# Zero-padded transposed probabilities in two half copies, and score masks in the scores' own tiles

## The chip, the cores and the metric

One NeuronCore of a Trainium2 chip runs the whole program. The metric is device time in microseconds (us), the median of the runs shown. Engines are named as the profile names them: PE is TensorE (PEld its weight loads), DVE VectorE, ACT ScalarE, POOL GpSimd, SP the engine that issues most DMAs. L540 is line 540 of the kernel before.

## The reference, cut to what matters

A "macaron" block on x of shape (2, 1024, 128): half an attention/feed-forward stack, a linear recurrence, half the same stack again. A stack has six layers, each of them

```
qkv = shift(x) @ Wqkv            # 16 heads of 64
q, k = l2norm and rotary tables
sim  = q . k over a window: 32 queries see their own 32 keys and the 32 before them
sim  = where(mask, -max, sim)    # no key after the query, none more than 32 before it
attn = softmax(sim)              # over 64 keys
x    = (attn @ v) @ Wo + x
x    = ffn(shift(x)) + x
```

A tile is 128 positions, which is four windows of 32. There are 16 tiles and 12 layers over the two stacks, so 192 tile-layers. Everything here is float32, except the mask and the identity that brings it in (`idb`), which are bfloat16.

## The kernel before, in words

Each engine runs its own program, unrolled over about 198 steps. In step s the tile-layer s-1 is projected (L_QKV), s-2 has its q and k transposed, its values computed and its scores taken (L_S), s-3 its softmax and the transposition of the probabilities (L_SM), s-4 its attention product and output projection (L_AV, L_WO), s-5 and s-6 its feed-forward (L_F, L_F2). The order inside a step is written out by hand for every engine; engines meet only through semaphores. `k.wait(sem, lag)` waits until `sem` has counted the tile of that lag.

The order on PE in one step is: projections 1 and 0 (L482), transposition of q (`tps`, L493), the attention product (`attend`, L540), projections 2 and 3, transposition of k, output projection (L593), transposition of the probabilities (L601), of the feed-forward's input (L606), the second feed-forward product (L621), the values (L488, second one after DVE's third rotation, L866), transposition of the next x (L639), the first feed-forward product (L501), the mask products (L517), the scores (L525).

The parts that the change touches:

- **Scores.** For each of 8 pairs of heads, two window halves `ty`, two windows `g` and two heads `hp` there is a product of 64 rows of contraction by 32 columns of output, so that it occupies one of eight 64x32 tiles of the array. They add onto a mask which two bfloat16 products of full 128x128 size (`idb` against a mask of 512 columns, one for each `ty`) have written to the two banks of `sps` before.
- **Probabilities.** After the softmax eight transpositions put them into PSUM (`tps`), partitions being keys (0 to 63 of one window pair, 64 to 127 of the other), and ACT copies all of it to `pT` in SBUF (L721).
- **Attention product.** 64 products of 64 rows by 64 columns, the moving operand 32 columns wide, take `pT` against the values (`va`) or the values shifted by one window (`vb`); the two window halves `t` go to two banks of `ops`. ACT copies `ops` to `oT` in another order (L695).
- **Next x.** PE transposes it into `tps` (slot 4; slot 5 for the recurrence's input) and waits before it for ACT's copies of k and of the probabilities, which read `tps`.
- **DVE's order.** Within a step: rotations, sums, the inverse square root in twelve small pieces (L815 to L847), between which it adds to `Z` (L968, L978), then the work of the recurrence in between the stacks (`middle`, 16 tiles only), then `hT` (L990, after ACT's gelu `fg`), then the maximum and subtraction of the scores (L997, L1000).
- **Instructions.** Every float32 product is recorded as two pairs of a weight load and a matmul, so the 64 products of `attend` and the 64 of `scores` are 128 pairs each in a step. PE's program is fetched by a DMA queue of its own (q8).

Of the kernel before, what the change touches and what calls it, by code (L numbers as in the profile page):

```python
# [21 lines left out]
P = 128  # L22
DEPTH, HEADS, DH, WIN = 6, 16, 64, 32
# [34 lines left out]
def macaron(nc, x_in, w_in, w_out, b_out, w_qkv, q_scale, k_scale, w_o,  # L58
            w_1, w_2, b_2, c_cols, c_rope, c_mask, c_ident, out):
    with ExitStack() as ctx:  # L60
# [13 lines left out]
        qT = sb("qT", [PAIRS, P])  # L74

        prob = sb("prob", [PAIRS, 2, 2 * WIN])
        pT = sb("pT", [PAIRS, P])
        oT = sb("oT", [PAIRS, P])
        va = sb("va", [2, INNER])
        vb = sb("vb", [INNER])  # L80
# [58 lines left out]
        d_vb = sem("d_vb")  # L139
        d_out = sem("d_out")  # L140
        c_zero, c_zero2 = sem("c_zero"), sem("c_zero2")
        s_idb, s_mask = sem("s_idb"), sem("s_mask")
        c_kf, c_scl = sem("c_kf"), sem("c_scl")
        c_sig = sem("c_sig")
# [321 lines left out]
        def _(pe):  # L466
# [45 lines left out]
            def scores(k):  # L512
                first = k.off("first", L_S, lambda u: ((POS - 1 - u % POS) // (POS - 1)) * 512)
                par = k.parity(L_S)
                for ty in range(2):
                    m = mask[:, bass.ds(first, 512)] if ty == 0 else mask[:, 0:512]
                    mm(sps[:, ty, :], idb[:, :], m, start=True, stop=False, skip_group_check=True)  # L517
                for p in range(PAIRS):
                    for ty in range(2):
                        for g in range(2):  # L520
                            for hp in range(2):
                                w = 2 * ty + g
                                at, rows = par * P + w * WIN, slice(hp * DH, (hp + 1) * DH)
                                to = (2 * g + (hp ^ ty)) * WIN
                                last = mm(sps[to:to + WIN, ty, p * 64:(p + 1) * 64], qT[rows, p, w * WIN:(w + 1) * WIN],  # L525
                                          kT[rows, p, at:at + 2 * WIN], start=False, stop=True, skip_group_check=True)
                last.then_inc(p_S, 1)

            def attend(k):
                par = k.parity(L_AV)  # L530
                for p in range(PAIRS):
                    for g in range(2):
                        for hp in range(2):
                            for t in range(2):
                                o4 = ops[:, t, p * 64:(p + 1) * 64].rearrange("p (g i) -> p g i", g=2)
                                at = (2 * p + hp) * DH
                                rows = slice(t * DH, (t + 1) * DH)
                                v = vb[rows, at:at + DH] if g == 0 else va[rows, par, at:at + DH]
                                to = (2 * g + (hp ^ t)) * WIN
                                last = mm(o4[hp * DH:(hp + 1) * DH, g, :], v, pT[rows, p, to:to + WIN],  # L540
                                          start=True, stop=True, skip_group_check=True)
                last.then_inc(p_O, 1)

            def step(k):
# [13 lines left out]
                    idle(4)  # L558
                if k.on(L_AV):
                    k.wait(a_pT, L_AV)  # L560
                    k.wait(d_vb, L_AV, per=32)
                    k.wait(v_z1, L_WO + 1)
                    k.wait(v_z, L_F2 + 1, base=TILES)
                    k.wait_mid(m_bh, M_IN + 1)
                    k.wait_mid(m_x2, M_OUT + 1)
# [63 lines left out]
                    k.wait(v_ab[2], L_QKV)  # L629
                    values(k, 0)  # L630
                if k.on(L_X):
                    k.wait(a_kT, L_S)
                    k.wait(a_pT, L_SM)
                    if k.mid(M_T) is not None:
                        k.wait_mid(m_xn, M_T)
                        tr(tps[:, 5, :], mx_n[:, :], idf[:, :])
                    k.wait(v_z, L_X)
                    k.wait_mid(m_z, TILES)
                    tr(tps[:, 4, :], Z[:, bass.ds(k.slot(L_X), P)], idf[:, :]).then_inc(p_xT, 1)  # L639
                if k.on(L_F):  # L640
                    k.wait(a_xnT, L_F)
                    if k.s == L_F:
# [25 lines left out]
        def _(act):  # L668
# [10 lines left out]
            def step(k):  # L679
                if k.on(L_QKV):  # L680
                    k.wait(v_red[0], L_QKV + 1)
                    square(k, 1)
                    square(k, 0)
                if k.on(L_SM):
                    k.wait(v_sub, L_SM)
                    fn(prob[:, :, :, :], prob[:, :, :, :], ACT.Exp).then_inc(a_exp, 1)
                if k.on(L_S):

                    k.wait(p_qT, L_S)
                    k.wait(p_S, L_S + 1)  # L690
                    cp(qT[:, :, :], tps[:, :, :]).then_inc(a_qT, 1)
                if k.on(L_AV):
                    k.wait(p_O, L_AV)
                    k.wait(p_wo, L_WO + 1)
                    cp(oT[:, :, :].rearrange("p a (t x) -> p t a x", t=2),  # L695
                       ops[:, :, :].rearrange("p t (a x) -> p t a x", x=2 * WIN)).then_inc(a_oT, 1)
                if k.on(L_QKV):
                    k.wait(v_red[1], L_QKV + 1)
                    square(k, 3)
                    square(k, 2)  # L700
                if k.on(L_S):
                    if k.parity(L_S) == 0:

                        k.wait(a_kT, L_S + 1)
                        k.wait(p_S, L_S + 1)
                        fl = k.off("flag", L_S, lambda u: u % TILES)
                        fn(kT[:, :, 0:WIN], kT[:, :, 2 * P:2 * P + WIN], ACT.Copy,
                           scale=kflag[:, bass.ds(fl, 1)]).then_inc(a_car, 1)
                    k.wait(p_kT, L_S)
                    k.wait(p_S, L_S + 1)  # L710
                    at = WIN + k.parity(L_S) * P
                    cp(kT[:, :, at:at + P], tps[:, :, :]).then_inc(a_kT, 1)
                if k.on(L_F):
                    k.wait(v_nb, L_F)
                    k.wait(p_xnT, L_F + 1)
                    fn(xn[:, :], xs2[:, :], ACT.Identity, bias=nb[:, 0:1], scale=rt2[:, 1:2]).then_inc(a_xn, 1)
                if k.on(L_SM):

                    k.wait(p_pT, L_SM)
                    k.wait(p_O, L_AV)  # L720
                    cp(pT[:, :, :], tps[:, :, :]).then_inc(a_pT, 1)  # L721
                if k.on(L_F):
                    k.wait(p_xnT, L_F)
                    k.wait(p_f[0], L_F + 1)
                    n = k.layer(L_F, 1)
                    fn(xnT[:, :], sps[:, 1, 0:P], ACT.Identity, bias=cols[:, RAW_B + n:RAW_B + n + 1],
                       scale=cols[:, RAW_G + n:RAW_G + n + 1]).then_inc(a_xnT, 1)
                if k.on(L_S):
                    k.wait(p_O, L_S + 2)
                    k.wait(d_vb, L_S + 1, per=32)  # L730
                    values(k, 1)
                    values(k, 0)
                if k.on(L_F):
                    k.wait(p_f[1], L_F)
                    k.wait(v_h, L_F + 1)
                    at = k.layer(L_F, 2)
                    for c in range(3):
                        rows = min(FC, FH - c * FC)
                        last = fn(fg[0:rows, c, :], proj[0:rows, 1, c * P:(c + 1) * P], ACT.Gelu,  # L739
                                  bias=cols[0:rows, bass.ds(at + c * 2 * DEPTH + 1, 1)])  # L740
                    last.then_inc(a_gelu, 1)
                if k.on(L_X):
                    k.wait(p_xT, L_X)
                    k.wait(p_v[0], L_X + 2)
                    hf, par = P // 2, k.parity(L_X)
                    cp(xsT[0:hf, par, 0:P], tps[0:hf, 4, :])
                    cp(xsT[hf:P, par, 1:P + 1], tps[hf:P, 4, :])
                    k.wait(a_xT, L_X + 1)
                    fn(xsT[hf:P, par, 0:1], xsT[hf:P, 1 - par, P:P + 1], ACT.Copy,
                       scale=0.0 if k.tile(L_X) % POS == 0 else 1.0).then_inc(a_xT, 1)  # L750
                if k.mid(M_T) is not None:

                    k.wait(p_xT, L_X)
                    cp(mx_t[:, :], tps[:, 5, :]).then_inc(m_xT, 1)

            def between(s):

# [24 lines left out]
        def _(dve):  # L782
# [135 lines left out]
            def step(k):  # L918
# [60 lines left out]
                if k.on(L_QKV):  # L979
                    for n in (8, 10, 11, 12):  # L980
                        rsqrt(k, n)
                middle(k)
                if k.on(L_F):
                    k.wait(p_f[0], L_F)
# [57 lines left out]
        def _(pool):  # L1042
# [99 lines left out]

            def between(s):

                if s in (1, 2):
                    outer_pow(1 + s)
                if s == 1:
# [26 lines left out]
def _constants():  # L1174
# [13 lines left out]
    rope = kinds.reshape(4, POS, P, DH).transpose(2, 0, 1, 3).reshape(P, 4 * POS * DH).astype(f)  # L1188

    row = np.arange(P)  # L1190
    i, g = (row % WIN)[:, None], (row // (2 * WIN))[:, None]
    j = (np.arange(512) % (2 * WIN))[None, :]
    usual = ((j < WIN) & (j >= i)) | ((j >= WIN) & (j - WIN <= i))
    first = np.where(g == 0, usual & (j >= WIN), usual)
# [22 lines left out]
```

## Time and profile before

| | |
|---|---|
| median of 3 runs | 3309.44 us (3306.02 to 3310.67) |
| the profiled execution's own time | 3317.88 us |
| its span, first to last instruction | 3316.0 us |
| busy share of the span | PE 96%, PEld 72%, DVE 83%, ACT 77%, POOL 67% |
| mean granted clock of TensorE | 0.995 of full speed |
| PE's two costliest helpers here | L540 378.6 + 376.7 us, L525 302.9 us |

A busy share is an average over stages: about 165 steps do only the layers' work, some 16 in the middle of the program do the recurrence besides, and the first and last few fill and drain the pipeline. Idle time is put before the instruction that waited, with the engine and line that ended it; "issue" means that nothing in the profile ended it.

### The profile page before, as it was taken

What the parts mean: (1) busy time and instruction counts of PE and PEld (TensorE: products, weight loads), DVE (VectorE), ACT (ScalarE), POOL (GpSimd) and SP (SyncE); (2) the same over time, 40 slices, a digit from 0 to 9 for tenths busy, and PEclk for the clock granted to TensorE, in tenths of its full rate; (3) what the DMA queues carried; (4) which work ended last, traced back from release to release, by engine and by line L of the source; (5) the groups of instructions that cost most, each with busy time, mean ns of one, the idle gap of its engine ahead of it and who ended that gap; (6) DMA issues with size and microseconds to landing.
All of it is one profiled execution on the core that took longest, in us unless ns stands there. A gap on an engine that the chain in (4) does not pass through costs nothing. (4 is left out here: it accounts for less than half of the span.)

```text
span 3316.0 us, 150147 instructions
## 1 busy us (share of the span) xinstructions
PE 3177.3 (96%) x63272; PEld 2384.7 (72%) x63464; DVE 2748.5 (83%) x6951; ACT 2545.5 (77%) x4144; POOL 2226.4 (67%) x1453
## 2 busy tenths in 40 slices
PE   7999999999999999999999999999999999999997
PEld 4777777777777777777777777777777777777776
DVE  7888888888888888889998888888888888888885
ACT  3777777777777777777777777777777777777775
POOL 6666666666666666667887666666666666666663
PEclk9999999999999999999999999999999999999999
DMA  4111111111111111111111111111111111111111
GB/s 124 45 48 45 48 44 48 45 48 45 47 42 43 48 45 48 45 48 45 47 39 45 48 44 48 45 46 41 45 48 45 48 44 48 45 44 43 47 52 38
DMA packets 135089, 157.39 MB, mean 47 GB/s; under 512 B 75539, under 2 KB 108439, under 8 KB 134423
## 3 DMA queue, kind: packets, MB, share of 16 engines
q1 hardware_dynamic: 129815, 144.42, 15.7%
q8 instruction: 509, 8.34, 1.1%
q10 hardware_dynamic: 4608, 3.34, 0.3%
q14 instruction: 157, 1.29, 0.1%
HBM read 33.38 MB, written 1.05 MB: 10 GB/s over the span
## 5 line engine op out<-in xcount | busy, mean ns | idle before, releaser
L1073 POOL TENSOR_TENSOR rot<-rot,swp 128x1024 f32<-128x1024 f32 x384 | 907.0, 2362 | 137.8 <-DVE rot L866 137.8
L482 PE MATMUL proj<-wq,xsT 128*128 128x512 f32 x1536 | 769.6, 622 | 27.6 <-DVE rot L866 10.3
L673 ACT ACTIVATE sq<-proj 128x512 f32<-128x512 f32 x768 | 438.0, 596 | 416.1 <-PE proj L482 406.3
L1082 POOL TENSOR_TENSOR rot<-rot,rn 128x1024 f32<-128x1024 f32 x384 | 724.4, 1908 | 0.0
L1063 POOL TENSOR_TENSOR rt<-rt,half 128x1 f32<-128x1 f32 x192 | 105.3, 549 | 755.6 <-DVE rt L936 755.6
L860 DVE TENSOR_TENSOR swp<-proj,tab 128x512 f32<-128x512 f32 x768 | 521.3, 679 | 12.2 <-ACT sq L673 7.2
L866 DVE TENSOR_TENSOR rot<-proj,tab 128x512 f32<-128x512 f32 x768 | 517.9, 674 | 0.8 <-PE tps L493 0.8
L990 DVE SCALAR_TENSOR_TENSOR hT<-proj,cols,fg 114x128 f32<-114x128 f32 (+1 forms) x576 | 166.7, 345 | 417.7 <-ACT fg L739 413.6
L493 PEld LDWEIGHTS tps<-idf,rot 128*128 128x128 f32 x3072 | 360.2, 141 | 206.2 <-issue 204.1
L1067 POOL TENSOR_TENSOR prob<-prob,rr 128x1024 f32<-128x1024 f32 x192 | 365.4, 1903 | 174.9 <-DVE rr L948 174.9
L482 PEld LDWEIGHTS proj<-wq,xsT 128*128 128x128 f32 x1536 | 259.8, 190 | 254.9 <-issue 145.4
L493 PE MATMUL tps<-idf,rot 128*128 128x128 f32 x3072 | 399.2, 273 | 2.8 <-POOL rot L1082 1.9
L540 PE MATMUL ops<-pT,vb 64*64 64x32 f32 x12288 | 378.6, 220 | 5.1 <-issue 4.9
L540 PE MATMUL ops<-pT,va 64*64 64x32 f32 x12288 | 376.7, 219 | 2.5 <-issue 2.3
L593 PE MATMUL ops<-wo,oT 128*128 128x128 f32 x3072 | 376.2, 276 | 2.4 <-ACT oT L695 2.4
L525 PEld LDWEIGHTS sps<-kT,qT 64*32 64x32 f32 x24576 | 260.0, 105 | 163.2 <-issue 163.0
L525 PE MATMUL sps<-kT,qT 64*32 64x64 f32 x24576 | 302.9, 225 | 71.6 <-issue 71.4
L488 PE MATMUL proj<-wq,xsT 128*128 128x512 f32 x768 | 367.8, 600 | 3.4 <-DVE rot L866 3.3
L593 PEld LDWEIGHTS ops<-wo,oT 128*128 128x128 f32 x3072 | 359.6, 193 | 2.7 <-issue 2.6
L540 PEld LDWEIGHTS ops<-pT,vb 64*64 64x64 f32 x12288 | 329.2, 134 | 38.2 <-issue 38.0
L721 ACT COPY pT<-tps 128x1024 f32<-128x1024 f32 x192 | 194.4, 1013 | 186.4 <-PE tps L601 186.4
L540 PEld LDWEIGHTS ops<-pT,va 64*64 64x64 f32 x12288 | 331.4, 135 | 3.2 <-issue 2.7
(102 smaller groups left out, 5873.0 us busy)
## 6 DMA issues: line engine op xcount, KB each, us to landing
vb<-va SPq DMA_DIRECT2D x192, 384.0 KB, 3.5
vb<-va SPq DMA_DIRECT2D x192, 128.0 KB, 3.6
wq<-in_L_ffn_Wqkv SPq DMA_DIRECT2D x95, 192.0 KB, 3.4
xs<-Z SPq DMA_DIRECT2D x192, 32.0 KB
wo<-in_L_ffn_Wo SPq DMA_DIRECT2D x94, 64.0 KB, 2.8
xs<-Z SPq DMA_DIRECT2D x192, 28.0 KB
xs<-Z SPq DMA_DIRECT2D x192, 3.8 KB
xs<-Z SPq DMA_DIRECT2D x192, 0.2 KB
```

Of the source, the lines that this page charges most:

```text
L482: mm(proj[:, c % 2, :], xsT[:, k.parity(L_QKV), 0:P], wq2[:, bass.ds(w + c * 512, 512)], start=True, stop=True).then_inc(p_qkv[c], 1)
L488: mm(proj[:, c, :], xsT[:, k.parity(L_S), 0:P], wq2[:, bass.ds(w + (4 + c) * 512, 512)], start=True, stop=True).then_inc(p_v[c], 1)
L493: last = tr(tps[:, p, :], rot[:, g * INNER + p * P:g * INNER + (p + 1) * P], idf[:, :])
L525: last = mm(sps[to:to + WIN, ty, p * 64:(p + 1) * 64], qT[rows, p, w * WIN:(w + 1) * WIN], kT[rows, p, at:at + 2 * WIN], start=False, stop ...
L540: last = mm(o4[hp * DH:(hp + 1) * DH, g, :], v, pT[rows, p, to:to + WIN], start=True, stop=True, skip_group_check=True)
L593: last = mm(ops[:, 0, 0:P], oT[:, p, :], wo[:, bass.ds(w + p * P, P)], start=(p == 0), stop=(p == PAIRS - 1))
L673: fn(sq[:, c * 512:(c + 1) * 512], proj[:, c % 2, :], ACT.Square).then_inc(a_sq[c], 1)
L860: v.tensor_tensor(halves(swp[:, c * 512:(c + 1) * 512]), swapped, tab[:, bass.ds(po + (2 * g + 1) * POS * DH, DH)] .rearrange("p (a d) -> ...
L866: v.tensor_tensor(heads(rot[:, c * 512:(c + 1) * 512]), heads(src), tab[:, bass.ds(po + 2 * g * POS * DH, DH)].unsqueeze(1) .to_broadcast( ...
L1067: g_.tensor_tensor(pr, pr, rr[:, :].unsqueeze(2).to_broadcast([P, HEADS, 2 * WIN]), ALU.mult).then_inc(g_nrm, 1)
L1073: g_.tensor_tensor(r, r, swp[:, g * INNER:(g + 1) * INNER], ALU.add).then_inc(g_add[g], 1)
L1082: g_.tensor_tensor(r, r, rn[:, g * HEADS:(g + 1) * HEADS].unsqueeze(2) .to_broadcast([P, HEADS, DH]), ALU.mult).then_inc(g_nm[g], 1)
```

## The change

The transposed probabilities get a buffer of twice the size, `pT[pair and g, hp, t, i]`. For half t = 0 only the partitions 0 to 63 are written, for t = 1 only 64 to 127, and the rest stays zero from one memset by POOL at the start. ACT copies the lower half of the partitions, DVE the upper half (in a new place, between the last piece of the inverse square root and `middle`), so that neither copy touches the zeros. Each product of `attend` then contracts over all 128 partitions and has a moving operand of 64 columns, the zeros cancelling what does not belong to it: 32 products of 128 rows by 64 columns instead of 64 of 64 by 64. PE waits for both copies. `ops` is filled in the order of `oT`. The next x is transposed into `ops` instead of `tps`, and PE waits for DVE's addition to `Z` instead of ACT's copies before it. The mask is written by eight products of 64 rows by 32 columns, each 512 wide, and the constant's rows are numbered to match.

```diff
-        pT = sb("pT", [PAIRS, P])
+        pT = sb("pT", [PAIRS * 2, 2, 2, WIN])
...
                 for ty in range(2):
                     m = mask[:, bass.ds(first, 512)] if ty == 0 else mask[:, 0:512]
-                    mm(sps[:, ty, :], idb[:, :], m, start=True, stop=False, skip_group_check=True)
+                    for g in range(2):
+                        for hp in range(2):
+                            rows, of = slice(hp * DH, (hp + 1) * DH), hp * DH + g * WIN
+                            to = (2 * g + (hp ^ ty)) * WIN
+                            mm(sps[to:to + WIN, ty, :], idb[rows, of:of + WIN], m[rows, :], start=True, stop=False,
+                               skip_group_check=True)
...
                 for p in range(PAIRS):
+                    o4 = ops[:, p // 4, (p % 4) * P:(p % 4 + 1) * P].rearrange("p (t g i) -> p t g i", t=2, g=2)
                     for g in range(2):
                         for hp in range(2):
-                            for t in range(2):
-                                o4 = ops[:, t, p * 64:(p + 1) * 64].rearrange("p (g i) -> p g i", g=2)
-                                at = (2 * p + hp) * DH
-                                rows = slice(t * DH, (t + 1) * DH)
-                                v = vb[rows, at:at + DH] if g == 0 else va[rows, par, at:at + DH]
-                                to = (2 * g + (hp ^ t)) * WIN
-                                last = mm(o4[hp * DH:(hp + 1) * DH, g, :], v, pT[rows, p, to:to + WIN],
-                                          start=True, stop=True, skip_group_check=True)
+                            at = (2 * p + hp) * DH
+                            v = vb[:, at:at + DH] if g == 0 else va[:, par, at:at + DH]
+                            last = mm(o4[hp * DH:(hp + 1) * DH, :, g, :], v,
+                                      pT[:, 2 * p + g, hp, :, :].rearrange("p t i -> p (t i)"),
+                                      start=True, stop=True, skip_group_check=True)
...
                     k.wait(a_pT, L_AV)
+                    k.wait(v_pT, L_AV)
...
                 if k.on(L_X):
-                    k.wait(a_kT, L_S)
-                    k.wait(a_pT, L_SM)
+                    k.wait(v_z1, L_WO)
...
-                    tr(tps[:, 4, :], Z[:, bass.ds(k.slot(L_X), P)], idf[:, :]).then_inc(p_xT, 1)
+                    tr(ops[:, 0, P:2 * P], Z[:, bass.ds(k.slot(L_X), P)], idf[:, :]).then_inc(p_xT, 1)
...
-                    cp(pT[:, :, :], tps[:, :, :]).then_inc(a_pT, 1)
+                    if k.s == L_SM:
+                        act.wait_ge(c_pz, 1)
+                    cp(pT[0:DH, :, :, 0, :], tps[0:DH, :, :].rearrange("p c (g h i) -> p (c g) h i", g=2, i=WIN)).then_inc(a_pT, 1)
...
                     for n in (8, 10, 11, 12):
                         rsqrt(k, n)
+                if k.on(L_SM):
+
+                    if k.s == L_SM:
+                        dve.wait_ge(c_pz, 1)
+                    k.wait(p_pT, L_SM)
+                    k.wait(p_O, L_AV)
+                    src = tps[DH:P, :, :]
+                    swapped = bass.AP(src.tensor, src.offset + WIN,
+                                      [list(src.ap[0]), [2 * WIN, 2 * PAIRS], [-WIN, 2], [1, WIN]])
+                    v.tensor_copy(pT[DH:P, :, :, 1, :], swapped).then_inc(v_pT, 1)
                 middle(k)
...
+                if s == 0:
+                    g_.memset(pT[:, :, :, :, :], 0.0).then_inc(c_pz, 1)
```

## Rows read from the trace of the kernel before

**Rows 1.** The page, part 1: busy us, share of span, instructions.
```profile
PE 3177.3 (96%) x63272; PEld 2384.7 (72%) x63464; DVE 2748.5 (83%) x6951; ACT 2545.5 (77%) x4144; POOL 2226.4 (67%) x1453
```
**Rows 2.** Waits of the whole run: who waited <- for whom: us in total, times, longest.
```profile
DVE hT L990 <- ACT fg L739: 413.6, 179, 4.2
...
PEld proj L488 <- DVE rot L866: 96.4, 189, 1.1
DVE mx L997 <- PE sps L525: 71.4, 70, 3.9
```
**Rows 3.** Timeline of DVE, ordinary step: start us, us, [idle before <-releaser].
```profile
835.24 0.87 DVE L990 SCALAR_TENSOR_TENSOR hT<-proj,cols,fg 114x128 f32<-114x128 f32 x3 [2.31 <-ACT fg L739]
...
846.82 0.68 DVE L866 TENSOR_TENSOR rot<-proj,tab 128x512 f32<-128x512 f32 x1
...
847.51 0.28 DVE L968 TENSOR_TENSOR Z<-Z,ops 128x128 f32<-128x128 f32 x1
...
849.11 0.19 DVE L847 SCALAR_TENSOR_TENSOR rn<-rt,sps 128x32 f32<-128x32 f32 x1
851.66 0.61 DVE L990 SCALAR_TENSOR_TENSOR hT<-proj,cols,fg 114x128 f32<-114x128 f32 x2 [2.36 <-ACT fg L739]
```
**Rows 4.** Timeline of ACT, the same step.
```profile
846.28 1.01 ACT L721 COPY pT<-tps 128x1024 f32<-128x1024 f32 x1 [0.81 <-PE tps L601]
...
848.78 0.59 ACT L677 COPY va<-proj 128x512 f32<-128x512 f32 x1 [0.19 <-PE proj L488]
849.38 1.28 ACT L739 ACT_TABLE_LOAD   x1
```
**Rows 5.** Timeline of PE, the same step and the one before.
```profile
830.38 1.93 PE L488 MATMUL proj<-wq,xsT 128*128 128x512 f32 x4
...
834.26 1.48 PE L525 MATMUL sps<-kT,qT 64*32 64x64 f32 x128
...
838.61 0.32 PE L540 MATMUL ops<-pT,vb 64*64 64x32 f32 x8
...
840.61 0.70 PE L482 MATMUL proj<-wq,xsT 128*128 128x512 f32 x1
...
846.86 1.88 PE L488 MATMUL proj<-wq,xsT 128*128 128x512 f32 x4
...
848.73 1.60 PE L501 MATMUL proj<-xnT,w 128*114 128x128 f32 x12
...
850.69 1.48 PE L525 MATMUL sps<-kT,qT 64*32 64x64 f32 x123
```
**Rows 6.** Timeline of PE, scores of a stalled step; then the page's instruction queue.
```profile
2416.27 1.28 PE L525 MATMUL sps<-kT,qT 64*32 64x64 f32 x104
2419.08 0.43 PE L525 MATMUL sps<-kT,qT 64*32 64x64 f32 x24 [1.53 <-issue]
...
q8 instruction: 509, 8.34, 1.1%
```
**Rows 7.** The recurrence's stretch: stage busy times; DVE's longest wait there.
```profile
1543.00:1825.00 282.00, 272.05 (x5342) 205.54 (x5357) 269.54 (x702) 215.50 (x358) 226.16 (x184) 1.00 0.16 44
...
DVE hT L990 <- ACT fg L739: 6.4, 5, 1.5
```
**Rows 8.** Groups by line: busy us, mean ns of one | idle before.
```profile
L540 PEld LDWEIGHTS ops<-pT,va 64*64 64x64 f32 x12288 | 331.4, 135 | 3.2 <-issue 2.7
L525 PEld LDWEIGHTS sps<-kT,qT 64*32 64x32 f32 x24576 | 260.0, 105 | 163.2 <-issue 163.0
L860 DVE TENSOR_TENSOR swp<-proj,tab 128x512 f32<-128x512 f32 x768 | 521.3, 679 | 12.2 <-ACT sq L673 7.2 <-issue 4.9
L1000 DVE TENSOR_TENSOR prob<-sps,mx 128x1024 f32<-128x1024 f32 x192 | 235.0, 1224 | 6.6
L1015 DVE MEMSET va<- 128x1024 f32 x1 | 0.9, 912 | 0.2 <-issue 0.2
L1126 POOL MEMSET hT<- 128x384 f32 x1 | 0.4, 417 | 0.0
```

More of the change, by code:

```diff
@@ L141, in macaron @@
         c_zero, c_zero2 = sem("c_zero"), sem("c_zero2")
+        c_pz = sem("c_pz")
+        v_pT = sem("v_pT")
         s_idb, s_mask = sem("s_idb"), sem("s_mask")
@@ L631, in step @@
                 if k.on(L_X):
-                    k.wait(a_kT, L_S)
-                    k.wait(a_pT, L_SM)
+                    k.wait(v_z1, L_WO)
                     if k.mid(M_T) is not None:
                         k.wait_mid(m_xn, M_T)
-                        tr(tps[:, 5, :], mx_n[:, :], idf[:, :])
+                        tr(ops[:, 0, 2 * P:3 * P], mx_n[:, :], idf[:, :])
                     k.wait(v_z, L_X)
                     k.wait_mid(m_z, TILES)
-                    tr(tps[:, 4, :], Z[:, bass.ds(k.slot(L_X), P)], idf[:, :]).then_inc(p_xT, 1)
+                    tr(ops[:, 0, P:2 * P], Z[:, bass.ds(k.slot(L_X), P)], idf[:, :]).then_inc(p_xT, 1)
                 if k.on(L_F):
@@ L694, in step @@
                     k.wait(p_wo, L_WO + 1)
-                    cp(oT[:, :, :].rearrange("p a (t x) -> p t a x", t=2),
-                       ops[:, :, :].rearrange("p t (a x) -> p t a x", x=2 * WIN)).then_inc(a_oT, 1)
+                    cp(oT[:, :, :], ops[:, :, :].rearrange("p b (a x) -> p (b a) x", x=P)).then_inc(a_oT, 1)
                 if k.on(L_QKV):
@@ L745, in step @@
                     hf, par = P // 2, k.parity(L_X)
-                    cp(xsT[0:hf, par, 0:P], tps[0:hf, 4, :])
-                    cp(xsT[hf:P, par, 1:P + 1], tps[hf:P, 4, :])
+                    cp(xsT[0:hf, par, 0:P], ops[0:hf, 0, P:2 * P])
+                    cp(xsT[hf:P, par, 1:P + 1], ops[hf:P, 0, P:2 * P])
                     k.wait(a_xT, L_X + 1)
@@ L753, in step @@
                     k.wait(p_xT, L_X)
-                    cp(mx_t[:, :], tps[:, 5, :]).then_inc(m_xT, 1)
+                    cp(mx_t[:, :], ops[:, 0, 2 * P:3 * P]).then_inc(m_xT, 1)
             def between(s):
@@ L1190, in _constants @@
     row = np.arange(P)
-    i, g = (row % WIN)[:, None], (row // (2 * WIN))[:, None]
+    i, g = (row % WIN)[:, None], (row // WIN % 2)[:, None]
     j = (np.arange(512) % (2 * WIN))[None, :]
```

## The prediction

> **What bounds the kernel now.** The page comes first: PE is busy 96% of the span, DVE 83%, ACT 77% [rows 1]. That looks like a PE bound, but a high share does not say which engine's delay would be paid back, so I read the waits next. DVE idles 413.6 us before `hT`, 179 times 2.3 us, always for ACT's gelu; PE's load for the second values product waits 189 times for DVE's rotation L866; DVE waits 70 times for the scores [rows 2]. The reader is to see a ring there: DVE waits for ACT, PE waits for DVE.
>
> The timeline of one ordinary step closes it. From the start of `hT` (835.24) DVE works to the end of rotation L866 (846.82 + 0.68 = 847.50): 12.26 us [rows 3]. The second values product follows and ACT starts to copy it at 848.78, 1.28 us later; the table load follows at 849.38 [rows 4], and the next `hT` starts at 851.66, 2.88 us after the copy began. The sum is 16.42, the distance of the two `hT`: this ring has no slack in it. PE is nearly as tight. Its values group takes 1.88 us when PE never stops and 1.93 when DVE was late [rows 5]; I count 129 steps of the first kind and 44 of the second. So PE and the ring DVE - PE values - ACT - DVE are within some 0.06 us of each other (unstalled steps are 16.36 at the shortest and 16.43 on average), and a gain on PE alone is worth at most that.
>
> Two other stages exist. First, in about every third ordinary step the scores stop in the middle, with no releaser but "issue": 104 of 128 pairs, 1.53 us of nothing, then the other 24 [rows 6]. PE's instructions come in 509 packets of 16.4 KB on their own queue [rows 6], 256 instructions of 64 bytes each; a scores burst is 256 instructions in 1.48 us, so nearly each burst crosses one packet's end, and in the stalls that I looked at it stops between pairs 79 and 125. DVE waits for these stalls: 71.4 us over 70 steps [rows 2]. Second, the recurrence's stretch of 282 us: DVE is busy 269.54 us of it, and waits for gelu only 5 times [rows 7]. At 17.6 us a step these are 16 steps, and in 11 of them DVE has no pause at all: DVE bounds them.
>
> **The attention product.** Before: from 838.61 to the next projection at 840.61, 2.0 us for 128 pairs [rows 5], of which the pairs come 8 in 0.117 us, 14.6 ns each, 58 ns for each of the four tiles. What paces them is the weight load: it grows from 105 to 135 ns from 32 to 64 columns [rows 8], 0.9 ns a column, 57 ns for 64, while a moving column takes (1.88 - 0.60) / 3 / 512 = 0.83 ns [rows 5], 27 ns for 32. After: 64 pairs, loads of 64 columns as before (57 ns), products of 64 columns (53 ns), so the wider product still fits behind the load; but only two tiles work side by side. 64 x 58 / 2 = 1.87 us. Half the instructions, the same time. I take 0. The condition is that a load still hides behind the product in front of it on the same rows. The bounds: 1.7 us (53 ns and nothing else) and, with load and product one after the other in each column half, 64 x 110 / 2 = 3.5 us, +1.65 a step.
>
> The Trainium skill ("TensorE: Matmul & The Clock Gate", Part 3, The mechanism) says that loads overlap running matmuls only when the row group differs; today neighbouring products alternate between the two row groups, afterwards all use the same rows. By it the 3.5 us would hold. The trace speaks against it where all 128 rows are in use: twelve pairs of L501 take 1.60 us, 0.12 us a pair, when product alone needs 0.107. It is a rival below.
>
> **The masks.** Before: the last L501 product starts at 848.73 + 1.60 - 0.28 = 850.05, the scores at 850.69 [rows 5]; less the usual 0.11, the masks cost 0.53 us: two passes of 512 bfloat16 columns (0.21 each) and 0.1 for the change to small tiles. After: eight products in eight different tiles. That such tiles work side by side is in the scores: 128 pairs in 1.48 us, 10 ns apart [rows 5], each 53 ns long, so more than five at a time. So 0.1 + 0.21 + 8 x 0.005 = 0.35, a gain of 0.18; if only the four of one bank run together, 0.53 again and nothing; one after the other, 1.8 us, +1.3 a step. I take -0.18 on PE. The ring does not contain the masks, so of it only the 0.06 us by which unstalled steps exceed the ring is paid, over some 96 of them: at most 6 us, taken as -4. In a stalled step it is paid nothing: what ends the stall is a packet's arrival, which an earlier start does not move.
>
> The skill ("TensorEngine Tiling (Array Packing)", Key Properties) has that a change of tiling mode drains the array. The trace shows about 0.1 us for one, and their number in a step stays two here.
>
> **The stalls.** Per step PE loses 128 instructions and gains 12, of about 679 (509 x 256 / 192, [rows 6]). One could hope that fewer instructions mean fewer stalls. But what counts is whether a packet ends late in the scores' own burst, which stays dense and gets 12 longer. Positions move by 563 - 512 = 51 instructions from step to step instead of 167, but spread as evenly; 70 stalls in some 165 steps says that 42% of the positions are bad; 12 more of 256 makes it up to 47%. So -0 to +8 us, taken as +4.
>
> **The copies of p.** ACT's takes half the partitions but as many elements in each, so 1.01 us as before [rows 4]: 0. DVE's is new: 1024 elements from PSUM. Below, the memset of 1024 elements, 0.91; above, two of the swapped-order reads of 512, 1.36; nearest, the 1024-element read of `sps`, 1.22 [rows 8]. I take 1.2. In an ordinary step it begins at 849.3, after L847 [rows 3], with p long transposed (ACT's copy began at 846.28 [rows 4]), and ends at 850.5; gelu releases DVE at 851.6. It costs nothing, and 1.1 us of cover is left. In the 11 steps without a pause it costs its whole length: 13 us (10 to 15). In the four neighbours where the pause is about 0.9, 1 us in all. Sum +14.
>
> **The rest.** The wait for `Z` (done at 847.79 [rows 3]) stands before x's transposition, which comes after the second values product, itself released by the rotation that ends 0.3 us earlier and 0.85 us long: hidden. What is queued behind it is L501 and the scores; it has some 0.3 us. `attend`'s new wait is for a copy that ended over 3 us before. POOL's memset is 2048 elements, 384 took 0.417 [rows 8], so up to 2.2 us once, before POOL has rotations to add: 0 to 2. `oT`'s copy only changes its order. Together +1.
>
> **Sum.** +14 (middle) + 4 (stalls) - 4 (masks) + 1 = +15 us. From the profiled execution's 3317.88 that gives 3333; this execution lies 8.4 above the median, and the shift goes to it unchanged: 3309.4 + 15 = 3324.5 us.
>
> **Rivals.**
> 1. The stalls go away with the instructions. For it: 18% fewer packets, and PE's ring of packets gains time over a whole step. Against it: the burst that runs dry is the scores, not `attend` (which hardly stalls). Half to all of the 71.4 us [rows 2] gone: 3254 to 3289. Chance 0.16.
> 2. PE's relief is paid in full, since PE's own 96% is the bound and the ring only looks closed: 0.18 x 96 = 17 to 0.18 x 150 = 27 us off, against +19: 3298 to 3312, 3304. For it: two thirds of the steps show the continuous 1.88. Against: the ring adds up with no rest. Chance 0.16.
> 3. Loads don't hide behind products in 128x64 tiles. Place: `attend`; it decides from about 0.3 us a step, PE's relief and gaps used up. Full price 1.65 - 0.3 = 1.3 us in some 150 ordinary steps: 3309 + 15 + 200 = 3525; half hidden, 3410. Against: today's 58 ns with loads of 57, and L501. Chance 0.15.
> 4. The masks don't run side by side, so that the change does not do what it says: four at a time gives the forecast within 4 us and is in it; two at a time costs 0.3 us a step, 3370. Chance 0.03.
>
> **Numbers.** The forecast has 0.50, 3314 to 3334 for itself. What a measurement here can tell from no change is 0.2%, 6.6 us. Faster by more: rival 1 and a third of rival 2, 0.21. Within: the rest of rival 2 and the low edge of the forecast, 0.16. Slower: 0.63. The range for 8 in 10 leaves out half of rival 1 below and most of rival 3 above: 3278 to 3370.
>
> **What would show it.** Right: DVE's pause before `hT` shrinks from 2.3 to about 1.2 us in ordinary steps and their distance stays 16.4; the recurrence's steps go from 17.6 to 18.8; `attend` takes 1.9 to 2.0 us in half the pairs; the scores begin 0.45 us after L501's last product; DVE still waits some 70 us for the scores. Wrong: `attend` over 2.3 us, DVE's wait for the scores under 40 us, or ordinary steps under 16.3.

## The result, and the profile after

The changed kernel takes 3320.84 us (median of 6 runs, 3319.98 to 3326.79), the kernel before 3308.28 beside it (6 runs, 3306.02 to 3310.67). The ratio is 1.0043, with an interval of 1.0033 to 1.0053: 14 us slower by the ratio, 12.6 by the medians. The forecast was +15. The sum is right, but two of its terms, the stalls and the steps around the recurrence, are far off and cancel; most of what follows is about them.

The two profiled executions are 3320.66 and 3317.88 us. The second lies 9.6 above the median of its kernel, so differences between these two traces understate the change by about that. The page, part 1, and the instruction queue, against [rows 1, 6]:

```profile
PE 3151.4 (95%) x52328; PEld 2382.6 (72%) x52328; DVE 2996.6 (90%) x7143; ACT 2543.0 (77%) x4144; POOL 2229.8 (67%) x1454
...
q8 instruction: 422, 6.91, 0.9%
```

DVE has 248 us more work: 192 copies of 1.23 us and some longer instructions. PE's packets fell from 509 to 422. The waits of the whole run, against [rows 2]:

```profile
DVE hT L1006 <- issue: 179.5, 164, 3.0
...
PE sps L532 <- issue: 68.2, 56, 2.2
...
DVE mx L1013 <- PE sps L532: 52.0, 50, 3.2
...
PE proj L484 <- ACT xsT L755: 41.9, 126, 1.0
```

The pause before `hT` fell from 2.3 to 1.1 us (its releaser is now unnamed; by the program's order it is still gelu, which ACT ends just before). DVE waits 50 times for the scores, not 70. PE has a new wait, for ACT's copy of x, 0.33 us each: this is where the time goes that the shorter masks gave back. It stands 106 to 132 times in the traces of all four kernels with short masks (the changed one, e1, e3, e4), and once or twice in those of before, e2 and e5, whose masks are long. An ordinary step on DVE (start, us, [idle before]), against [rows 3]:

```profile
829.24 1.23 DVE L997 COPY pT<-tps 64x1024 f32<-64x1024 f32 x1
...
831.87 0.87 DVE L1006 SCALAR_TENSOR_TENSOR hT<-proj,cols,fg 114x128 f32<-114x128 f32 x3 [1.40 <-issue]
```

And on PE, against [rows 5]:

```profile
832.14 1.95 PE L484 MATMUL proj<-wq,xsT 128*128 128x512 f32 x4 [0.34 <-ACT xsT L755]
...
834.90 0.34 PE L544 MATMUL ops<-pT,vb 128*64 128x64 f32 x4
...
836.91 2.04 PE L484 MATMUL proj<-wq,xsT 128*128 128x512 f32 x4
...
845.27 1.64 PE L503 MATMUL proj<-xnT,w 128*114 128x128 f32 x12
846.84 0.41 PE L523 MATMUL sps<-mask,idb 64*32 64x512 bf16 x8
847.07 1.44 PE L532 MATMUL sps<-kT,qT 64*32 64x64 f32 x127
849.97 0.21 PE L532 MATMUL sps<-kT,qT 64*32 64x64 f32 x1 [1.46 <-issue]
```

`attend` runs from 834.90 to 836.91: 2.0 us, the time that twice the pairs took before. The last product of L503 starts at 845.27 + 1.64 - 0.28 = 846.63 and the scores at 847.07, 0.44 us later. The last row is a stall again, at pair 127.

Now the recurrence. DVE, a POOL row and PE of one of its steps:

```profile
1632.05 1.23 DVE L997 COPY pT<-tps 64x1024 f32<-64x1024 f32 x1
...
1633.84 1.25 DVE L894 SCALAR_TENSOR_TENSOR xb<-Z,xb 128x128 f32<-128x128 f32 x1
...
1637.42 0.87 DVE L1006 SCALAR_TENSOR_TENSOR hT<-proj,cols,fg 114x128 f32<-114x128 f32 x3
```
```profile
1633.03 3.82 POOL L1098 TENSOR_TENSOR rot<-rot,rn 128x1024 f32<-128x1024 f32 x2
```
```profile
1636.73 0.32 PE L532 MATMUL sps<-kT,qT 64*32 64x64 f32 x8 [1.41 <-issue]
1636.97 1.13 PE L484 MATMUL proj<-wq,xsT 128*128 128x512 f32 x2
1638.35 1.68 PE L484 MATMUL proj<-wq,xsT 128*128 128x512 f32 x2 [0.24 <-DVE hT L1006]
1639.82 1.91 PE L495 MATMUL tps<-idf,rot 128*128 128x128 f32 x8
```

Three things happen there. First, the copy stands in full on DVE, which has no pause before `hT`. Second, behind it L894 takes 1.25 us. Here are its groups in the kernel before, in the changed one, and in one with the copy later (e4_copy_late), each over the eleven steps in which DVE has no pause:

```profile
L888 DVE SCALAR_TENSOR_TENSOR xb<-Z,xb 128x128 f32<-128x128 f32 x11 | 3.9, 354 | 0.0
```
```profile
L894 DVE SCALAR_TENSOR_TENSOR xb<-Z,xb 128x128 f32<-128x128 f32 x11 | 13.8, 1251 | 0.0
```
```profile
L894 DVE SCALAR_TENSOR_TENSOR xb<-Z,xb 128x128 f32<-128x128 f32 x11 | 3.9, 354 | 0.0
L998 DVE COPY pT<-tps 64x1024 f32<-64x1024 f32 x17 | 20.9, 1228 | 0.5
```

The same instruction is 0.90 us longer where the copy has pushed it under POOL's L1098 (1633.03 to 1636.85). It runs in five more steps before these, so the whole run says more; the same three kernels again, all 16 steps:

```profile
L888 DVE SCALAR_TENSOR_TENSOR xb<-Z,xb 128x128 f32<-128x128 f32 x16 | 8.0, 497 | 0.0
```
```profile
L894 DVE SCALAR_TENSOR_TENSOR xb<-Z,xb 128x128 f32<-128x128 f32 x16 | 22.1, 1381 | 0.1
```
```profile
L894 DVE SCALAR_TENSOR_TENSOR xb<-Z,xb 128x128 f32<-128x128 f32 x16 | 7.7, 483 | 0.0
```

The change costs 14.1 us here. The scan of the same steps (L901, now L907) gives a little back: 26.6 us in all before, 25.3 after.

Third, PE, which now waits for `hT`, does its next eight transpositions in 1.91 us, not 1.04; the stage table (PE, PEld, DVE, ACT, POOL busy; granted clock; DMA share, GB/s) of the whole stretch and of these 3 us:

```profile
1545.00:1850.00 305.00, 279.21 (x4433) 208.60 (x4433) 298.21 (x718) 216.27 (x359) 225.41 (x183) 0.98 0.15 40
1639.00:1642.00 3.00, 3.00 (x16) 2.04 (x16) 2.60 (x5) 1.91 (x3) 0.97 (x2) 0.50 0.02 5
```

The granted clock is 0.50 there, the 1.2 GHz level; it fell after PE had idled 1.41 us in a stall and 0.24 us for `hT`, the first and third of its rows above. Four transposition groups are at that level in the stretch and a fifth at 1540.9, just ahead of it; the kernel before has none there.

The Trainium skill ("SBUF — State Buffer", Who interferes with whom) states that a DVE instruction with two inputs in SBUF contends with a GpSimd instruction that reads SBUF, and that the ports they share are an exclusive lock. The trace agrees: both inputs of L894 are in SBUF, the first of L1098's two instructions ends at 1633.03 + 1.91 = 1634.94, and L894 ends 0.15 us after that, at 1635.09. This is no single case. In the kernel before, the changed one and e4, all 48 executions of this addition begin under a POOL instruction and end 0.14 to 0.15 us after that one ends, and all 48 scans 0.28 us after theirs. So the 0.354 us of before are not undisturbed either: the addition began there in the last 0.2 us of L1073, and the copy pushed it past that end and under the next instruction, L1098. The same addition at L1010 (L1026), where POOL has nothing to do, takes 0.27 us. The copy reads PSUM and stays at 1.23 there and elsewhere.

To compare kernels I use the distance between the starts of two `mx` reductions on DVE: 163 ordinary steps and 23 around the recurrence. A step of at most 16.8 us counts as without a stall, a longer one as stalled; the means of the first kind are given, and of some of the second.

```
kernel                ordinary, us   without stall      stalled      23 middle steps, us
before                2755.2          94 of 16.48       69 of 17.5    398.8
changed               2729.6         118 of 16.44       45 of 17.5    429.0
e1_masks_only         2765.1          85 of 16.48       78            398.6
e2_no_masks           2709.6         138 of 16.44       25            427.8
e3_act_end            2723.5         125 of 16.43       38            395.2
e4_copy_late          2734.5         117                46            414.3
e5_best               2720.7         128 of 16.44       35            396.5
e8_copy_twice         2727.5         128 of 16.53       35            445.5
e9_narrow             2745.3          99 of 16.47       64 of 17.4    399.0
e10_six_tiny          2767.5          90 of 16.56       73 of 17.5    400.2
e11_act_both_early    2784.5          10, most others 16.8 to 17.1    400.2
```

So between these two traces the change took 26 us out of the ordinary steps, by fewer stalls, and put 30 into the middle. The trace of before is 9.6 us above its median, so the 26 is an upper value. e9_narrow below, whose trace lies on its median, is the better base: 16 us less in the ordinary steps.

### The profile page after: what moved, and what is told of

Same layout as the page of the kernel before. It is cut to its first block and busy times, and to the rows that moved or that the text cites. A ratio compares the mean times of both kernels' runs of the same rounds, so it can differ in the third digit from the quotient of the medians.

```text
span 3318.9 us, 128450 instructions
## 1 busy us (share of the span) xinstructions
PE 3151.4 (95%) x52328; PEld 2382.6 (72%) x52328; DVE 2996.6 (90%) x7143; ACT 2543.0 (77%) x4144; POOL 2229.8 (67%) x1454
## 5 line engine op out<-in xcount | busy, mean ns | idle before, releaser
L1098 POOL TENSOR_TENSOR rot<-rot,rn 128x1024 f32<-128x1024 f32 x384 | 724.8, 1911 | 0.0
L544 PE MATMUL ops<-pT,vb 128*64 128x64 f32 x6144 | 378.8, 225 | 0.0
L544 PE MATMUL ops<-pT,va 128*64 128x64 f32 x6144 | 369.0, 222 | 0.0
L532 PEld LDWEIGHTS sps<-kT,qT 64*32 64x32 f32 x24576 | 284.8, 105 | 86.5 <-issue 76.0
L727 ACT COPY pT<-tps 64x1024 f32<-64x1024 f32 x192 | 193.2, 1006 | 185.5 <-PE tps L607 185.5
L544 PEld LDWEIGHTS ops<-pT,vb 128*64 128x64 f32 x6144 | 311.2, 138 | 33.1 <-issue 32.9
L503 PEld LDWEIGHTS proj<-xnT,w 128*114 128x114 f32 (+1 forms) x2304 | 273.9, 178 | 74.2 <-issue 67.6
```

The lines of the kernel that those rows point to most:

```text
L544: last = mm(o4[hp * DH:(hp + 1) * DH, :, g, :], v, pT[:, 2 * p + g, hp, :, :].rearrange("p t i -> p (t i)"), start=True, stop=True, skip_g ...
L1098: g_.tensor_tensor(r, r, rn[:, g * HEADS:(g + 1) * HEADS].unsqueeze(2) .to_broadcast([P, HEADS, DH]), ALU.mult).then_inc(g_nm[g], 1)
```

## The experiments

Each ratio is to runs of the kernel before on the same chip. A difference between two kernels is the difference of their ratios times 3308.

**e1_masks_only**: the kernel before with the eight masks (and the constant's row numbering for them).

```
+ for g in range(2):
+     for hp in range(2):
+         ... mm(sps[to:to + WIN, ty, :], idb[rows, of:of + WIN], m[rows, :], ...)
- mm(sps[:, ty, :], idb[:, :], m, ...)
```

> The kernel before with the eight small mask products and nothing else of the change (12 PE instructions more in a step). Theory (ring through DVE and ACT, packets of instructions that come late): the scores begin about 0.2 us earlier, the ring is not shortened, stalls in the scores stay at 65 to 75; 3303 to 3312 us. Rival (PE's relief is paid in full): 0.18 us in 96 to 150 steps, 3281 to 3291 us. Rival (the small masks bring the fewer stalls seen after the change): about 50 stalls, some 3290 us.

3326.24 us, 1.0050 (1.0036 to 1.0065): +17 us. My theory had it at no change or a small gain. The time is in stalls; waits and queue:

```profile
PE sps L530 <- issue: 91.9, 81, 2.4
...
DVE mx L1002 <- PE sps L530: 73.5, 67, 4.7
```
```profile
q8 instruction: 518, 8.49, 1.0%
```

PE stops 81 times for 91.9 us, before 68 times for 71.4. The steps without a stall stay at 16.48 us, so the shorter masks by themselves gain nothing.

**e2_no_masks**: the changed kernel with the two full-array masks of before.

```
- for g in range(2):
-     for hp in range(2):
-         ... mm(sps[to:to + WIN, ty, :], idb[rows, of:of + WIN], m[rows, :], ...)
+ mm(sps[:, ty, :], idb[:, :], m, ...)
```

> The changed kernel with the two full-size mask products of before. Theory (half the pairs in the attention product are what makes the instruction stalls fewer; the copies cost some 30 us around the recurrence): DVE waits for the scores about 50 times as after the change, steps of the recurrence stay at 19.5 to 20.3 us, 3319 to 3327 us. Rival (the masks brought the relief): back to 70 stalls, 3335 to 3345 us.

3304.0 us (12 runs), 0.9990 (0.9979 to 1.0001): 17.5 us below the changed kernel, so the small masks cost the same in both surroundings. Both theories are missed: 3319 to 3327 us assumed that the masks do nothing, and the stalls did not come back. Stalls:

```profile
PE sps L527 <- issue: 32.8, 35, 2.0
```

35 stalls are left, half of before's, with the masks of before. That points at `attend`'s saved instructions; the copies differ too, and e9_narrow separates them.

**e3_act_end**: the changed kernel with the upper copy on ACT, last in its step.

```
- (DVE, after rsqrt)   v.tensor_copy(pT[DH:P, :, :, 1, :], swapped).then_inc(v_pT, 1)
+ (ACT, after mx_t)    cp(pT[DH:P, :, :, 1, :], swapped).then_inc(v_pT, 1)
```

> The changed kernel, but ACT copies the upper half too, as the last thing in its step, in the 1.3 us in which it waits for the first projection; DVE has its old order. Theory (DVE's copy costs only where DVE has no pause, around the recurrence): those steps go back to 17.6 us, the stalls stay at about 50, 3283 to 3295 us, faster than both kernels. Rival (ACT's pause is too short: squares, exponentials and DVE's rotations come later): ordinary steps grow by 0.1 to 0.3 us, 3310 to 3340 us.

3283.15 us, 0.9934 (0.9913 to 0.9955): 36 us below the changed kernel. As expected, and more than my +14 for the middle can explain: its 23 middle steps are 34 us shorter, and the granted clock does not fall in them.

**e4_copy_late**: the changed kernel with DVE's copy behind `middle(k)` instead of in front.

```
+ middle(k)
  if k.on(L_SM):
      ...
      v.tensor_copy(pT[DH:P, :, :, 1, :], swapped).then_inc(v_pT, 1)
- middle(k)
```

> The changed kernel with DVE's copy placed behind the recurrence's instructions instead of in front of them. Theory (of the 1.9 to 2.7 us that a recurrence step grew, 1.2 are the copy, 0.9 are one addition with both sources in SBUF, L894, that was pushed under POOL's multiplication and takes 1.25 instead of 0.35 us): L894 takes 0.35 us again, those steps take 18.6 to 18.9 us, 3306 to 3314 us. Rival (the time goes wherever DVE meets POOL, in whichever instruction): another instruction grows by as much, 3318 to 3323 us.

3303.2 us (12 runs), 0.9984 (0.9973 to 0.9995): 20 us below the changed kernel for one line moved, a little more than expected (its trace is of its slowest run, 3313.86, so the two traces differ by 7 only). L894 is back at 354 ns in the eleven steps (above) with the 17 copies of 1.23 us still there. The middle is 14.7 us shorter. L894 accounts for 14.4 of it over 16 steps; the scan takes 1.3 back, and the clock falls in two steps instead of five. The collision with POOL is thereby shown.

**e5_best**: e3 and e2 together: wide product, full masks, the upper copy at the end of ACT's step.

```
- eight masks, copy on DVE
+ mm(sps[:, ty, :], idb[:, :], m, ...)
+ (ACT, last)   cp(pT[DH:P, :, :, 1, :], swapped).then_inc(v_pT, 1)
```

> Both halves copied by ACT (the upper one at the end of its step), the wide attention product, and the two full-size mask products of before. Theory (the wide product saves stalls, the small masks cost them, DVE's copy costs around the recurrence; the three add up): some 35 waits of DVE for the scores, recurrence steps at 17.6 us, 3266 to 3278 us. Rival (they don't add, because ACT's new copy takes up what the earlier scores would leave): 3280 to 3290 us.

3277.1 us (3276.12 to 3281.52), 0.9902 (0.9888 to 0.9917): 1% faster than the kernel before, faster than both. The time is as expected; DVE's waits for the scores are 47, not some 35. Waits, and the recurrence's stretch, against [rows 2, 7]:

```profile
DVE hT L998 <- ACT fg L740: 402.0, 176, 4.2
...
DVE mx L1005 <- PE sps L527: 47.6, 47, 4.2
...
PE sps L527 <- issue: 45.1, 46, 1.8
```
```profile
1543.00:1825.00 282.00, 272.64 (x4442) 205.62 (x4458) 268.66 (x700) 233.85 (x381) 227.05 (x184) 1.00 0.16 43
```

ACT has room at that place: the copy lies in its wait for the next projection.

```profile
843.90 0.99 ACT L762 COPY pT<-tps 64x1024 f32<-64x1024 f32 x1
...
845.28 0.60 ACT L673 ACTIVATE sq<-proj 128x512 f32<-128x512 f32 x1 [0.39 <-PE proj L484]
```

**e6_pad_attend** and **e7_pad_wo**: e2 with 128 waits on a semaphore long satisfied, in front of `attend` or of the output projection, to give PE its instructions back without work.

```
+ for _ in range(128):
+     pe.wait_ge(c_zero2, 1)
```

> e2_no_masks with 128 waits on an already reached semaphore in front of the attention product, so that PE's program has as many instructions per step as before the change. Theory (the number of PE instructions sets how often a packet is late): stalls in the scores return, every third step, about 65 to 75 waits of DVE and 65 to 75 us; the queue q8 shows about 509 packets. Rival (it was the dense burst of the attention product, not the count): stalls stay at about 35. If a wait costs PE time, the attention product starts later by 128 times its price, which the steps show apart from the stalls.

> The same 128 waits, but behind the transposition of k, in front of the output projection, 128 instructions nearer to the scores. Theory (count alone): as e6, 65 to 75 stalls. Rival (what matters is how many instructions lie between the packet boundary and the scores, so their place counts): clearly more or fewer than in e6, 30 or over 100.

4681.76 and 4731.98 us, one run each, at a granted clock of 0.863: inconclusive. The queue q8 holds 461 packets in both, not 509, and PE stops in the scores 45 times in the first and 31 in the second, in steps that are 7 us longer. A satisfied wait is not free; PE's row of the first:

```profile
2413.77 0.48 PE L541 MATMUL ops<-pT,vb 128*64 128x64 f32 x4 [5.53 <-issue]
```

5.53 us for 128 of them is 43 ns each; the median pause is 5.0 us in e6 and 5.5 in e7, 39 and 43 ns a wait. Behind them the granted clock is 0.50, and four pairs take 0.48 us, 0.34 above. The padding changes far more than the number of instructions.

**e8_copy_twice**: e2 with DVE's copy made a second time, into a scratch tile.

```
  v.tensor_copy(pT[DH:P, :, :, 1, :], swapped).then_inc(v_pT, 1)
+ k.wait(v_pT, L_SM + 1)
+ v.tensor_copy(dum[DH:P, :, :, :], swapped)
```

> e2_no_masks with DVE's copy of the upper half made twice, the first time into a buffer that nobody reads. Theory (an ordinary step has 1.1 us of cover left after the first copy, the second is 1.15): ordinary unstalled steps grow by 0.0 to 0.2 us, the recurrence's steps by 1.2 us each; 3304 + 20 to 30 + 0 to 25, that is 3325 to 3355 us. Rival (DVE's copy already costs in ordinary steps): ordinary steps grow by the full 1.15 us, 3480 us or more.

3340.56 us, 1.0093 (1.0076 to 1.0110), 34 us over e2. Steps without a stall grow by 0.09 us, the middle by 17.7: of the second 1.23 us an ordinary step hides 1.14. That is the cover of 1.1 us that the prediction said was left.

**e9_narrow**: e5 with the 128 narrow pairs of before in `attend`, on the padded `pT`.

```
+ for t in range(2):
+     rows = slice(t * DH, (t + 1) * DH)
+     ... mm(o4[hp * DH:(hp + 1) * DH, g, :], v, pT[rows, 2 * p + g, hp, t, :], ...)
- mm(o4[hp * DH:(hp + 1) * DH, :, g, :], v, pT[:, 2 * p + g, hp, :, :]..., ...)
```

> e5_best with the 64 narrow products of before in attend (64 rows by 64 columns, from the new buffer, which holds the same numbers), so 128 PE instructions more in a step and nothing else. Theory (the wide product gains by its count of instructions alone, as it takes the same 2.0 us): DVE's waits for the scores go from 47 to 65 to 75, in every third step, 3303 to 3313 us, as the kernel before. Rival (the gain of e5 came from the two copies or from x's new place in PSUM): about 47 waits, 3275 to 3283 us.

3312.54 us (11 runs), 1.0005 (0.9996 to 1.0014). e5 differs from it in the width of the product, and in the order in which `ops` is filled and ACT copies it out; that copy takes 1.016 us in both. e5 is 34 us faster. Both need 2.0 us for the product; the difference is again in the stalls:

```profile
PE sps L527 <- issue: 61.6, 63, 1.8
...
PE ops L541 <- issue: 9.1, 18, 1.7
```
```profile
q8 instruction: 509, 8.34, 1.1%
```

63 stalls in the scores (46 in e5), 18 in `attend` (1). And e9 against before says that two copies instead of one, at e5's places, cost 2 us, and at most 5.

**e10_six_tiny**: the kernel before with six one-column products, the 12 instructions that the small masks add, in front of `attend`.

```
+ for _ in range(6):
+     mm(ops[:, 1, 0:1], idb[:, :], idb[:, 0:1], start=True, stop=True, ...)
```

> The kernel before with six products of one column (12 PE instructions a step, as many as the small masks add) at the head of the attention product, overwritten by it. Theory (the masks cost by lying densely between the last packet boundary and the scores): 65 to 73 stalls as before, and at most 0.06 to 0.2 us a step for the products themselves, 3309 to 3325 us, with unstalled steps grown and not stalled ones more frequent. Rival (the count per step, by the pattern in which boundaries meet the scores): 76 to 84 stalled steps as in e1, unstalled ones unchanged.

3332.4 us, 1.0061 (1.0048 to 1.0074), above the 3309 to 3325 of my theory. 0.08 us more in each step without a stall accounts for some 15 us; the queue holds 518 packets, as e1's. Stalls:

```profile
PE sps L525 <- issue: 60.6, 61, 2.0
...
PE proj L482 <- issue: 11.2, 11, 1.5
```

Those in the scores are not more than before (68 for 71.4 us), where e1 had 81 for 91.9; a few appear at L482, behind `attend`. So 12 more instructions make the stalls of the scores more and longer when they stand directly in front of them (and the masks are 0.2 us shorter, as in e1), not when they stand elsewhere. Its own price muddies the total, and with one trace each I call this likely, not shown.

**e11_act_both_early**: e5 with ACT's second copy directly behind the first.

```
  cp(pT[0:DH, :, :, 0, :], tps[0:DH, ...]).then_inc(a_pT, 1)
+ cp(pT[DH:P, :, :, 1, :], swapped).then_inc(v_pT, 1)
  ...
- (ACT, last)   cp(pT[DH:P, :, :, 1, :], swapped).then_inc(v_pT, 1)
```

> e5_best with ACT's copy of the upper half directly behind that of the lower, before the feed-forward's input and the values. Theory (ACT's part of the ring begins at the copy of the values, and 0.34 us are free before it): ordinary unstalled steps grow by 0.4 to 0.9 us, 3350 to 3430 us. Rival (ACT has 17% idle time, so where the copy stands doesn't matter): within 5 us of e5.

3354.38 us, 1.0126 (1.0106 to 1.0147), 74 us over e5, as my theory had it, for one copy moved within an engine that is busy 81 to 83%. PE now waits for ACT's values copy in nearly every step, which delays gelu and the ring behind it:

```profile
PE proj L503 <- ACT va L677: 97.5, 174, 0.7
...
DVE hT L995 <- ACT fg L744: 477.9, 178, 4.6
```

**When a packet comes.** The DMA records of these traces, which none of the views above lists one by one, show each packet of q8. In the eleven kernels other than e6 and e7, at every one of the 623 places where PE stops inside the scores, it goes on 2.2 to 3.1 us after a packet began to move and 1.1 to 1.7 after it landed. So the stalls are late packets. From one packet's end to the next lie 124 pairs (997 pairs for 8 packets); an end between two stalls can be placed by counting. Stalls by the pair of the scores' burst at which a packet ends:

```
packet ends at pair     64 to 79    80 to 95    96 to 111   112 to 127
before                  1 of 21     23 of 25    20 of 21    20 of 24
e9_narrow               1 of 21     21 of 25    19 of 19    19 of 26
e5_best                 0 of 22      5 of 21    15 of 22    20 of 20
e1_masks_only          10 of 26     21 of 22    22 of 22    22 of 23
e10_six_tiny            0 of 24     18 of 22    19 of 20    21 of 24
```

The ends are spread evenly, as the prediction said. With fewer instructions a step (e5) most ends at pairs 80 to 95 no longer stall: there the fetch had mostly begun 3 to 5 us before PE arrived. With the small masks ends at pairs 64 to 79 begin to stall; with as many instructions elsewhere (e10) they do not.

## Why the prediction came out right, and where it was wrong

That the time came out right is luck: two wrong terms cancelled. One path of four steps leads from the kernel before to the changed one, in the prediction's terms:

```
edit                                     from -> to          measured   predicted
two copies of p, other small edits       before -> e9         +2        +1 for the rest
wide product in attend                   e9 -> e5            -34         0
upper copy on DVE, not at ACT's end      e5 -> e2            +29        +14
eight small masks                        e2 -> changed       +17        -4 by length, +4 by stalls
sum                                                          +14        +15
```

By other measures the wide product is worth 27 us (ordinary and middle steps of the traces of e9 and e5), the copy on DVE 36 (e3 to changed) and the masks 17 (before to e1) or 11 (e5 to e3); the intervals leave each some 7 us either way.

- **The ring.** Right. Steps without a stall went from 16.48 to 16.44 us although PE got its 0.18 us back, and what PE gained it now waits for ACT (126 waits, 0.33 us). With the long masks in the changed kernel (e2) they take 16.44 as well, and the short masks alone (e1) leave them at 16.48: even the -4 us that I gave the masks' length are not there. Rival 2, a relief of PE paid in full, is out: 0.18 a step would show as 16.30. (Its range should by its own numbers begin at 3301, not 3298.) e11 tests the same ring from ACT's side.
- **The attention product.** Right: 2.0 us for 64 pairs, 29 ns a pair in 128x64 tiles, with loads that I put at 57 ns. Rival 3 is out: with load and product one after the other it would be 3.5 us. The rule of the Trainium skill ("TensorE: Matmul & The Clock Gate", Part 3, The mechanism) that a load overlaps only where the row group differs does not hold for these products, which all use the same rows.
- **The length of the masks.** Right: 0.43 us from L503's last product to the scores in the median step (0.44 in the one shown), 0.45 forecast, 0.64 before. Eight tiles run side by side, and rival 4 is out.
- **The stalls, "+4".** Wrong, twice over. I let the frequency follow from the positions of packet ends alone: a packet that ends late in the scores' burst stalls it, however many instructions the rest of the step has. Then the wide product could not matter, and it is worth -34 us; rival 1, to which I gave 0.16, described what it does. DVE's waits for the scores went to 52 us, where I had named "some 70" as a sign of being right. A packet's end at the same pair stalls less often with fewer instructions in a step (the table above): stalled steps go from 64 to 35 of 163 (e9 to e5). And shorter masks in front of the burst were to be free. Two long masks are 4 instructions in 0.53 us, eight short ones 16 in 0.35; the second leave the packet on its way less time for more instructions used up, and cost +17. How the 17 divide between the shorter time and the twelve instructions no run separates.
- **The copy on DVE, "+14 middle".** The length (1.23 us; 1.2 forecast), the cover in ordinary steps (2.3 to 1.1 us of pause; the second copy of e8 fits almost to the hundredth) and the place (the steps around the recurrence) are right. The size is not: +30 in the middle of the traces, steps of 19.5 to 20.3 us and not 18.8. Missing were L894 under POOL's multiplication, 14.1 us over its 16 steps (the scan gave 1.3 back), shown by e4; and PE's idling for `hT`, with which the granted clock fell to 0.50 for 3 us in five of these steps. Those steps take 20.3 us, their neighbours 19.5, so some 4 us in all. 14 + 14.1 - 1.3 + 4 is 31, against 30 measured. That the idling for `hT` made the clock fall is argued from its place; e3 and e5, where DVE has no copy, have no fall in these steps. I had taken every duration on DVE as fixed while moving the work by 1.2 us; that holds only until an instruction slides under another engine's.

The errors are -34 for the product, +17 for the masks and +15 for the copy on DVE; they cancel. The forecast of the time is right; as an account of the change it is half right.

Open is what starts the fetch of a packet. The middle half of the fetches begins 0.6 to 2.0 us after PE has passed the end of the packet before (before and e9), and no more than 146 pairs ahead of need, so little more than one packet is fetched ahead; but some begin over 5 us after it. Why the fetch comes earlier with fewer instructions a step no run here separates. The padding that should have told it (e6, e7) was too expensive.

## What to carry to other kernels

Where PE's instructions are as short as 10 ns, count them: half the instructions in the same engine time were worth 1% here, and short masks with 12 more directly ahead of the densest burst cost half of one. Before adding work to an engine with a pause in most steps, look at the stage that has none, and at what its later instructions slide under on a neighbour's timeline; a place at the end of another engine's step may be free when the engine's busy share says the opposite (e5), and the same copy a few instructions earlier may cost 74 us (e11). A forecast that comes out right as a sum should still be taken apart by single edits.

## What the runs showed of the hardware that was not expected

- PE's instruction stream is a resource. 413 to 518 packets pass, and PE loses 33 (e2) to 92 us (e1) waiting in the scores alone. A packet takes 0.9 to 1.5 us to move, and PE goes on 2.2 to 3.1 us after it began. The Trainium skill ("Runtime: NRT & Kernel Launch", Instruction fetch mechanics) has the stream as blocks of 256 instructions, the next fetched while the current one runs, with the crossing of a block mostly hidden. The block size agrees: packet ends lie 124 pairs apart, which is 249 recorded instructions besides waits. The hiding does not, in bursts of 10 ns pairs.
- A semaphore wait that is already satisfied takes about 40 ns on PE (128 in 5.0 us in the median step of e6, in 5.5 in e7).
- The same DVE instruction, 128x128 from two SBUF tiles, takes 0.274 us beside an idle POOL, 0.354 in the tail of one of POOL's instructions and 1.251 early under one. It ends 0.15 us after POOL's, 48 times of 48. The scan beside it ends 0.28 us after: in the eleven steps it takes 2.13 us before, where both begin together, and 1.72 after, where it begins 0.5 us later. What such an instruction costs is set by where it lands on POOL's timeline.
- After 1.41 us of idle in a stall and 0.24 us for `hT`, the granted clock stood at 0.50, the 1.2 GHz level, over the 3 us from 1639 to 1642.
